# Sixteen-head landmark attention with a mixture of experts: the pseudo-inverse on a'a, the values carried through it

## The chip, the cores and the metric

One core of a Trainium2 chip runs the whole layer as one program. The metric is the device time of that core in microseconds. TensorE (PE) multiplies into PSUM, VectorE (DVE), ScalarE (ACT) and GpSimd (POOL) work beside it, and SyncE (SP) issues most transfers. The engines run their own instruction streams and meet only at semaphores.

## What is computed

The layer is an attention block and a mixture of eight experts, each with a norm ahead of it. The change lies in the attention, in the pseudo-inverse of a softmax matrix `attn2` of 64 x 64, one for each of 4 batches and 16 heads:

```python
def moore_penrose_inverse(a, iters=6):
    col = jnp.abs(a).sum(axis=-1); row = jnp.abs(a).sum(axis=-2)
    z = jnp.swapaxes(a, -1, -2) / (jnp.max(col) * jnp.max(row))
    for _ in range(iters):
        az = a @ z
        z = 0.25 * z @ (13 * I - az @ (15 * I - az @ (7 * I - az)))
    return z
...
attn2_inv = moore_penrose_inverse(attn2)
out = attn1 @ attn2_inv @ (attn3 @ v)
```

What is done with `attn1`, the convolution, the output product and the experts comes later in the program and isn't changed.

## The kernel before

The program has these stages: the norm of x and its transposes (to about 87 us of the profile); the landmarks and `c1`, 16 rounds of 4 heads in which sim3 is multiplied, its softmax taken and attn3 @ v built up (`c1_sim`, `c1_ut`, `c1_v3`, to 313 us); the pseudo-inverse (313 to 377 us); the landmark values and the products with w_fc and w_q (`landmark_values`, `g1_round`, 377 to 397.5 us); the token stage with softmax, convolution, output and routing (36 steps, from 397.5 us); the experts.

Two matrices of 64 x 64 lie over one another on the 128 partitions, so there are 32 pairs q, and a product of 64 x 64 uses one quarter of TensorE's array. The pairs are worked on in four groups of eight, and a turn of the iteration is four group steps, numbered n = 0 to 23. In the trace every product of fp32 operands has two records on PE and two on its weight load; counts of records are twice the counts of products.

The iteration of before keeps y = a z and w, the product of the factors, side by side in `yw`. For each n TensorE forms y y (`square`, 16 products of 64 columns), y (y y - 7 y + 15) (`cube`, the same) and factor times [y w] (`next_values`, 16 products of 128 columns), and `pair` interleaves the squares and cubes of two groups with the next values of the two groups before them. VectorE makes one pass over 512 elements per partition for each of `low_powers` (15 - 7 y, line 1054), `square` (line 1062) and `step_factor` (line 1068); ScalarE takes the next values out of PSUM in one instruction of 1024 elements (line 741). GpSimd does nothing in these turns. At the end `z_product` forms w zt, and `landmark_values` multiplies the values v3 with the inverse. The groups n and n + 1 use different banks of PSUM, and the order of every engine is written out by hand. GpSimd's stream is the all-reduce of the two maxima (line 553), the first w (line 556, waits for the first squares), four iotas (line 562), and the sum of `band` and `shift` (line 564) that the convolution of the token stage needs. `xd`, `band` and `shift` have nothing to do with the pseudo-inverse. `att`, the transposed `attn2`, is made in c1 at m = 4 and 5 by `a_transposed` (line 1512) and read by the squares of line 1563, ahead of `c1_ut(15, 0)`.

## Time and profile before

| | us |
|---|---|
| median of 3 runs | 1106.95 |
| range of the runs | 1105.58 to 1109.3 |
| span of the profiled execution | 1103.7 |
| median less span | 3.25 |
| PE busy in the span | 1063.5 |
| DVE, ACT, POOL busy | 644.0, 318.9, 300.6 |
| pseudo-inverse and landmark values, 313.4 to 397.5 | 84.1 |

The profile is one execution, with the time of every instruction. Busy times are shares of the span and an average over stages, so the stage that is changed is read by itself: its timeline by engine, and the view of busy time by stretch.

### The profile page before, as it was taken

Reading aid. Unit: us, or ns where it says so; the run is one execution under the profiler, and the core shown is the slowest. Engines: PE = TensorE matmul, PEld = TensorE weight load, DVE = VectorE, ACT = ScalarE, POOL = GpSimd, SP = SyncE. Lnnn points to the kernel's source line nnn. Section 1 sums busy time; section 2 is a strip of 40 time slices with the busy share of each in tenths; the row PEclk is TensorE's granted clock in tenths of the full one; section 3 lists DMA queues with packets and bytes.
Section 4 is the critical chain, followed back from the end, with each engine's and each line's share of the span. In section 5 each row is a group of like instructions: output and inputs, shape, how many; then the busy total and the mean of one; then the engine's idle time right before and its main releaser. Section 6 shows DMA issues by size and latency. Waiting matters only on the chain.

```text
span 1103.7 us, 22943 instructions
## 1 busy us (share of the span) xinstructions
PE 1063.5 (96%) x9126; PEld 854.5 (77%) x9126; DVE 644.0 (58%) x1376; ACT 318.9 (29%) x471; POOL 300.6 (27%) x303
## 2 busy tenths in 40 slices
PE   4999999999999999999999999999999999999996
PEld 4888888888888756666766766788887877878895
DVE  7457756565558576677677777875434334343332
ACT  4433233223324423322332332331222122121210
POOL 6000000000020013225525526563242333333333
PEclk9999999999999999999999999999999999999998
DMA  9300000000300050221422314335423233333122
GB/s 337 130 1 1 1 1 1 1 1 1 98 3 0 2 192 20 106 67 59 146 67 68 106 58 130 97 126 107 92 43 54 41 45 53 45 51 46 20 30 24
DMA packets 48252, 68.27 MB, mean 62 GB/s; under 512 B 8224, under 2 KB 41504, under 8 KB 47136
## 3 DMA queue, kind: packets, MB, share of 16 engines
q1 hardware_dynamic: 34288, 46.83, 13.7%
q0 software_dynamic: 13440, 16.93, 9.2%
q10 hardware_dynamic: 432, 3.24, 0.7%
q8 instruction: 62, 1.02, 0.4%
q14 instruction: 30, 0.25, 0.1%
HBM read 41.43 MB, written 26.59 MB: 62 GB/s over the span
## 4 chain that ended last, share of the span: by engine, by line
PE 84%; DVE 6%; issue 3%; POOL 3%; DMA 2%; ACT 1%; POOLq 0%; DVEq 0%; ACTq 0%
PE ps L1886 17%; PE ps L1482 10%; PE ps L1441 10%; PE ps L1785 9%; PE ps L1929 9%; PE ps L1732 8%; PE ps L1777 5%; PE ps L1870 2%; DMA out<-mem 2%; PE ps L1599 1%; PE ps L1849 1%; PE ps L1415 1%; PE ps L1618 1%; PE ps L1923 1%; PE ps L1497 1%
## 5 line engine op out<-in xcount | busy, mean ns | idle before, releaser
L1886 PE MATMUL ps<-mem 128*128 128x256 f32 (+1 forms) x1152 | 221.9, 345 | 0.0
L1886 PEld LDWEIGHTS ps<-mem 128*128 128x128 f32 x1152 | 190.1, 191 | 27.2 <-issue 7.5
L608 POOL DMA_INDIRECT out<-mem x60 | 101.8, 1697 | 187.9 <-DVE mem L1301 139.0
L1289 DVE TENSOR_TENSOR mem<-mem,ps 128x512 f32<-128x512 f32 x66 | 45.3, 687 | 147.3 <-PE ps L1886 129.6
L573 POOL TENSOR_TENSOR mem<-mem,small 128x1024 f32<-128x1024 f32 x36 | 68.7, 1907 | 223.9 <-DVE small L1223 119.4
L1732 PE MATMUL ps<-mem 128*128 128x512 f32 x288 | 129.4, 593 | 0.0
L821 ACT ACTIVATE mem<-ps 128x512 f32<-128x512 f32 x66 | 39.4, 597 | 275.5 <-PE ps L1886 247.4
L1785 PE MATMUL ps<-mem 128*128 128x256 f32 x512 | 118.4, 384 | 0.0
L1482 PE MATMUL ps<-mem 128*128 128x256 f32 x512 | 117.3, 382 | 0.6 <-ACT mem L695 0.6
L1441 PE MATMUL ps<-mem 128*128 128x256 f32 x512 | 114.7, 380 | 0.0
L1929 PE MATMUL ps<-mem 128*128 x480 | 113.7, 380 | 0.9 <-DVE mem L1289 0.9
L1785 PEld LDWEIGHTS ps<-mem 128*128 128x128 f32 x512 | 94.7, 190 | 14.7 <-issue 3.2
L1441 PEld LDWEIGHTS ps<-mem 128*128 128x128 f32 x512 | 95.5, 190 | 12.7 <-issue 0.3
L1482 PEld LDWEIGHTS ps<-mem 128*128 128x128 f32 x512 | 94.8, 190 | 13.5 <-issue 0.8
L1929 PEld LDWEIGHTS ps<-mem 128*128 128x128 f32 x480 | 88.3, 190 | 11.6 <-issue 1.1
L1732 PEld LDWEIGHTS ps<-mem 128*128 128x128 f32 x288 | 54.2, 190 | 54.8 <-issue 52.7
L587 POOL DMA_INDIRECT xs_d<-mem,idx x64 | 62.5, 977 | 54.3 <-DVE idx L1203 34.1
L1777 PEld LDWEIGHTS ps<-mem 128*64 128x64 f32 x1152 | 57.1, 137 | 20.7 <-issue 20.3
L1777 PE MATMUL ps<-mem 128*64 128x116 f32 x1152 | 65.1, 266 | 0.8 <-POOL mem L573 0.8
L1318 DVE COPY mem<-mem 128x2048 f32 x51 | 62.1, 1236 | 5.6 <-issue 3.2
L796 ACT ACTIVATE mem<-ps 128x928 f32<-128x928 f32 (+2 forms) x36 | 31.5, 875 | 111.5 <-PE ps L1777 111.5
L1301 DVE TENSOR_SCALAR mem<-ps,mem 128x256 f32<-128x256 f32 x66 | 29.7, 479 | 48.4 <-PE ps L1929 48.2
(239 smaller groups left out, 1382.1 us busy)
## 6 DMA issues: line engine op xcount, KB each, us to landing
mem<-w_gu SPq DMA_DIRECT2D x9, 1024.0 KB, 5.6
mem<-xs_d SPq DMA_DIRECT2D x22, 260.0 KB, 2.8
mem<-x SPq DMA_DIRECT2D x8, 512.0 KB, 8.2
mem<-x SPq DMA_DIRECT2D x32, 128.0 KB, 2.2
out<-mem SPq DMA_DIRECT2D x32, 128.0 KB, 1.7
mem<-w_down SPq DMA_DIRECT2D x8, 512.0 KB, 5.8
xnt_d<-mem ACTq DMA_DIRECT2D x3, 1056.0 KB, 5.2
mem<-xnt_d SPq DMA_DIRECT2D x3, 1056.0 KB, 6.2
```

Source lines behind the costliest of these rows:

```text
L573: pool.tensor_tensor(a1[:, u], ex[:, u].rearrange("p (h c) -> p h c", h=H), ri[:, 16 * u:16 * u + 16].unsqueeze(2).to_broadcast([P, H, M]) ...
L587: pool.indirect_dma_start(out=xs_d, out_offset=bass.IndirectOffsetOnAxis(ap=idx[:, u, v, c:c + 1].bitcast(U32), axis=0), in_=xd[:, u, v, c ...
L608: pool.indirect_dma_start(out=out_rows, out_offset=bass.IndirectOffsetOnAxis(ap=rows_to.bitcast(U32), axis=0), in_=ys[:, r % YRING], in_of ...
L1289: dve.tensor_tensor(hid[:, n % 2], sil[:, n % 2], bank(2 + n % 2), ALU.mult).then_inc(s("m_hid"), 1)
L1318: dve.tensor_copy(v, w_gu_s[:, e]).then_inc(s("m_w"), 1)
L1441: mm = pe.matmul(bank(t // 2)[:, t % 2 * 2 * P:(t % 2 + 1) * 2 * P], xnts[b][:, k, HALO + P * t:HALO + P * t + P], g3c[:, b, k, j * P:(j + ...
L1482: mm = pe.matmul(bank(6)[:, k * 2 * P:(k + 1) * 2 * P], xna[:, b, t, k * P:(k + 1) * P], e3s[m % 4][:, t], start=(t == 0), stop=(t == RT - 1))
L1732: mm = pe.matmul(bank(2 * u + half), xnt2[b % 2][:, k, TO * t:TO * t + P], g1c[:, b, k, 512 * half:512 * half + 512], start=(k == 0), stop ...
L1777: mm = pe.matmul(bank(4, 2)[c:c + 64, (h // 2) * P:(h // 2) * P + TO], a1[:, q % 2, h], band[:, h], start=True, stop=True)
L1785: mm = pe.matmul(bank(6)[:, 0:D], cvt[:, j, at_:at_ + P], pm[:, b, j], start=(j == 0), stop=(j == J - 1))
L1886: mm = pe.matmul(bank(2 * c + n % 2)[:, i * size:(i + 1) * size], w[:, k, c, f * P:(f + 1) * P], xst[:, a % 2, k, 0:size], start=(k == 0), ...
L1929: mm = pe.matmul(bank(down_bank(a, b))[:, 0:D], hid[:, u, i * size + b * P:i * size + (b + 1) * P], w_d_s[:, e, f], start=(f == 0), stop=( ...
```

## The change

The iteration now works on y = a'a (scaled), which needs no transpose, and on u = a' v3, the values, instead of w. With c = y - 3.5 (kept as `less`) a group step is two rounds of 16 products of 128 columns:

- `first(n)`: less times [y u], which gives y y - 3.5 y and the same for u. ScalarE takes it out in two instructions of 512, times 1/4, into `mw`, the y half first.
- `quadratic(n)`: VectorE makes `quad` = 4 times the y half of mw, plus 2.75, from SBUF to SBUF.
- `second(n)`: quad times mw.
- `next_values(n)`: VectorE sets yu = 27/32 yu - second in two passes of 512, the y half first, each with its own count in `i_yu`.
- GpSimd makes less for n + 4 from the y half, in one pass of 512, as soon as that half is counted.

It is the same polynomial: the quarter of (y y - 3.5 y + 2.75)(y y - 3.5 y) taken from 27/32 y is the quarter of y (13 - 15 y + 7 y y - y y y). In the last turn only the u half is formed, in products of 64 columns (`last_second`). Neither `z_product` nor the product with v3 is left; `landmark_values` transposes u.

In c1, `a_transposed` and its copies are gone; `column_sums` multiplies each a with one column of ones (64 products of 1 column) and VectorE takes the maximum from PSUM. The first squares move from m = 15 to m = 14. At m = 15 come `first_rows` (a' v3, 16 products of 64 columns for each of four groups, three of them here) and `first(0)` and `first(1)`.

The diff, cut:

```diff
+def last_bank(n):
+    return 2 if n == 4 * ITERS - 1 else 4 + 2 * (n % 2)
+
+
+def yu_count(n):
+    return 2 * min(n, 4 * (ITERS - 1)) + max(0, n - 4 * (ITERS - 1))
...
+        yu = at(SQ, 2 * HQ).rearrange("p (q c) -> p q c", q=NQ)
+        y_of, u_of = yu[:, :, 0:M], yu[:, :, M:2 * M]
+        mw = at(2 * SQ, 2 * 16 * M).rearrange("p (u q c) -> p u q c", u=2, q=8)
+        quad = at(2 * SQ + HQ, 2 * 8 * M).rearrange("p (u q c) -> p u q c", u=2, q=8)
+        less = at(3 * SQ, HQ).rearrange("p (q c) -> p q c", q=NQ)
...
-            pool.wait_ge(s("i_y0mm"), 4)
-            pool.tensor_scalar(w_of, eye1.unsqueeze(1).to_broadcast([P, NQ, M]), 1.0, 0.0, ALU.mult, ALU.add)\
-                .then_inc(s("i_w0"), 1)
+            for n in range(4 * ITERS):
+                gs = slice(8 * (n % 4), 8 * (n % 4) + 8)
+                if n < 4:
+                    pool.wait_ge(s("i_y0"), n + 1)
+                else:
+                    pool.wait_ge(s("i_yu"), 2 * (n - 4) + 1)
+                pool.tensor_tensor(less[:, gs], y_of[:, gs], eye_shift.unsqueeze(1).to_broadcast([P, 8, M]), ALU.subtract)\
+                    .then_inc(s("i_less"), 1)
 
...
+            def products_out(n):
+                act.wait_ge(s("i_first"), n + 1)
+                if n >= 2:
+                    act.wait_ge(s("i_second"), n - 1)
+                product = bank(2 * (n % 2), 2).rearrange("p (q c) -> p q c", q=8)
+                for c in (0, M):
+                    act.activation(mw[:, n % 2, :, c:c + M], product[:, :, c:c + M], ACT.Copy, scale=0.25).then_inc(s("i_mw"), 1)
...
+                if m == NP2 - 2:
+                    for g in range(4):
+                        first_values(g)
+            for g in range(3):
+                first_rows(g)
+            products_out(0)
+            products_out(1)
             c1_tokens_out(NP2 - 1)
-
-            for n in range(4 * ITERS):
...
-                act.wait_ge(s("i_zmm"), g + 1)
-                act.activation(zf[:, 8 * g:8 * g + 8], bank(g).rearrange("p (q c) -> p q c", q=8), ACT.Identity,
-                               scale=zz[:, 1:2]).then_inc(s("i_z"), 1)
+            products_out(2)
...
-                if m in (4, 5):
-                    b = 2 * (m - 4) + 1
-                    dve.wait_ge(s("b_at_tp"), b + 1)
-                    dve.tensor_copy(att[:, J * b:J * b + J], bank(7).rearrange("p (q c) -> p q c", q=J)).then_inc(s("b_at_dve"), 1)
+                if m == 4:
+                    dve.wait_ge(s("b_cols"), 1)
...
+            def quadratic(n):
+                dve.wait_ge(s("i_mw"), 2 * n + 1)
+                if n >= 2:
+                    dve.wait_ge(s("i_second"), n - 1)
+                dve.scalar_tensor_tensor(out=quad[:, n % 2], in0=mw[:, n % 2, :, 0:M], scalar=4.0,
+                                         in1=eye_quad.unsqueeze(1).to_broadcast([P, 8, M]),
+                                         op0=ALU.mult, op1=ALU.add).then_inc(s("i_quad"), 1)
+
+            def next_values(n):
                 gs = slice(8 * (n % 4), 8 * (n % 4) + 8)
...
+                dve.wait_ge(s("i_second"), n + 1)
+                product = bank(last_bank(n), 2).rearrange("p (q c) -> p q c", q=8)
+                for c in (0, M) if n < 4 * (ITERS - 1) else (M,):
+                    to = yu[:, gs, c:c + M]
+                    dve.scalar_tensor_tensor(out=to, in0=to, scalar=27.0 / 32, in1=product[:, :, c:c + M],
+                                             op0=ALU.mult, op1=ALU.subtract).then_inc(s("i_yu"), 1)
+
+            quadratic(0)
+            quadratic(1)
+            c1_values(NP2 - 1)
+            next_values(0)
+            for n in range(2, 4 * ITERS):
+                quadratic(n)
+                next_values(n - 1)
...
 
             dve.wait_ge(s("a_xnt_out"), 16 * (B - 1))
...
+            def column_sums():
+                pe.wait_ge(s("b_a"), B)
+                for q in range(NQ):
                     for r in halves:
-                        mm = pe.matmul(bank(6 + b % 2)[r, j * M:(j + 1) * M], zt[r, J * b + j], eye1[r], start=True, stop=True)
-                mm.then_inc(s("b_at_tp"), 1)
...
+            def first_rows(g):
+                pe.wait_ge(s("c1_v3"), 8 * g + 8)
+                for i in range(8):
+                    for r in halves:
+                        mm = pe.matmul(bank(g)[r, i * M:(i + 1) * M], zt[r, 8 * g + i], v3[r, 8 * g + i], start=True, stop=True)
+                mm.then_inc(s("i_u0mm"), 1)
...
+            spread = [i // 2 + 4 * (i % 2) for i in range(8)]
+
+            def crossed(h, i):
+                return halves[(h + i // 4) % 2]
+
+            def first(n):
+                for i in spread:
+                    q = 8 * (n % 4) + i
+                    for h in range(2):
+                        mm = pe.matmul(bank(2 * (n % 2), 2)[crossed(h, i), i * 2 * M:(i + 1) * 2 * M], less[halves[h], q],
+                                       yu[halves[h], q], start=True, stop=True)
+                mm.then_inc(s("i_first"), 1)
+
+            def second(n):
+                for i in spread:
+                    for h in range(2):
+                        mm = pe.matmul(bank(4 + 2 * (n % 2), 2)[crossed(h, i), i * 2 * M:(i + 1) * 2 * M], quad[halves[h], n % 2, i],
+                                       mw[halves[h], n % 2, i], start=True, stop=True)
+                mm.then_inc(s("i_second"), 1)
...
+            def last_second(n):
+                pe.wait_ge(s("i_mw"), 2 * n + 2)
+                pe.wait_ge(s("i_quad"), n + 1)
+                pe.wait_ge(s("i_yu"), yu_count(n - 1))
+                for i in spread:
+                    for h in range(2):
+                        mm = pe.matmul(bank(last_bank(n), 2)[crossed(h, i), (2 * i + 1) * M:(2 * i + 2) * M], quad[halves[h], n % 2, i],
+                                       mw[halves[h], n % 2, i, M:2 * M], start=True, stop=True)
+                mm.then_inc(s("i_second"), 1)
...
+            def turn(n, done):
+
+                wait_alone(pe, "i_less", done + n + 2)
+                first(n + 1)
+                wait_alone(pe, "i_mw", 2 * done + 2 * n + 2)
+                wait_alone(pe, "i_quad", done + n + 1)
+                wait_alone(pe, "i_yu", 2 * done + 2 * n - 2)
+                second(n)
...
-                    a_transposed(2 * m - 8)
-                    a_transposed(2 * m - 7)
+                if m == 4:
+                    column_sums()
                 if more:
                     c1_sim(2 * m + 5)
                 if m == 2:
                     pe.wait_ge(s("b_sub"), B)
...
+                if m == 4:
+                    pe.wait_ge(s("b_sums"), 1)
+                if m == NP2 - 2:
                     pe.wait_ge(s("c1_raw"), 2 * NP2)
                     for g in range(4):
-                        for i in range(8):
-                            for r in halves:
-                                mm = pe.matmul(bank(g)[r, i * M:(i + 1) * M], att[r, 8 * g + i], att[r, 8 * g + i], start=True, stop=True)
-                        mm.then_inc(s("i_y0mm"), 1)
-                if not last:
+                        first_square(g)
+                if m == NP2 - 1:
+                    pe.wait_ge(s("i_y0"), 4)
+                    for g in range(3):
+                        first_rows(g)
+                if m != NP2 - 2:
                     c1_sum_columns(m - 1)
                     c1_v3(m - 1)
                 c1_ut(m, 0)
                 if more and m > 1:
                     c1_max_columns(m + 2)
...
+                if m == NP2 - 1:
+                    c1_sum_columns(m)
+                    for n in range(2):
+                        pe.wait_ge(s("i_u0"), n + 2)
+                        first_ready(n)
...
+            second(0)
+            c1_v3(NP2 - 1)
+            first_ready(2)
+            first(2)
+            pe.wait_ge(s("i_mw"), 4)
+            first_rows(3)
+            pe.wait_ge(s("i_quad"), 2)
+            second(1)
+            pe.wait_ge(s("i_u0"), 4)
+            turn(2, 0)
+            turn(3, 0)
+            with pe.Fori(0, ITERS - 2) as it:
+                for n in range(4, 8):
+                    turn(n, 4 * it)
+            for n in range(4 * (ITERS - 1), 4 * ITERS - 1):
+                first_ready(n + 1)
+                first(n + 1)
+                last_second(n)
...
+            for n in range(4 * (ITERS - 1), 4 * ITERS - 1):
+                first_ready(n + 1)
+                first(n + 1)
+                last_second(n)
+            pe.wait_ge(s("w_in"), 16 * 3)
...
-            pe.wait_ge(s("w_in"), 16 * 3)
+            pe.wait_ge(s("i_yu"), yu_count(4 * ITERS - 2))
+            g1_round(0)
             landmark_values(0)
+            last_second(4 * ITERS - 1)
```

The order on the engines. VectorE in the steady part, before: three kinds of passes, of two groups at a time (1062 reads PSUM and SBUF, 1068 PSUM and the constants `eyes`, 1054 SBUF and `eyes`).

```order
L1062 TENSOR_TENSOR mem<-ps,mem 128x512 [waits i_squaremm,i_low] x2
L1068 SCALAR_TENSOR_TENSOR mem<-ps,eyes 128x512 [waits i_cubemm]
L1054 SCALAR_TENSOR_TENSOR mem<-mem,eyes 128x512 [waits i_yw]
L1068 SCALAR_TENSOR_TENSOR mem<-ps,eyes 128x512 [waits i_cubemm]
L1054 SCALAR_TENSOR_TENSOR mem<-mem,eyes 128x512 [waits i_yw]
```

VectorE in the same part, now: `quadratic` is line 1065 (SBUF and `eyes`, both in SBUF), `next_values` line 1075 (SBUF and PSUM).

```order
L1065 SCALAR_TENSOR_TENSOR mem<-mem,eyes 128x512 [waits i_second,i_mw]
L1075 SCALAR_TENSOR_TENSOR mem<-mem,ps 128x8x64 [waits i_second]
L1075 SCALAR_TENSOR_TENSOR mem<-mem,ps 128x8x64
L1065 SCALAR_TENSOR_TENSOR mem<-mem,eyes 128x512 [waits i_second,i_mw]
L1075 SCALAR_TENSOR_TENSOR mem<-mem,ps 128x8x64 [waits i_second]
L1075 SCALAR_TENSOR_TENSOR mem<-mem,ps 128x8x64
```

Three passes for a group step stand there as before; two of them are now the two halves of the last step.

GpSimd between the all-reduce and the token stage, before (`ISA` is no arithmetic):

```order
L556 TENSOR_SCALAR mem<-eyes 128x32x64 [waits i_y0mm]
L562 IOTA mem 128x8 [waits band_in]
L562 IOTA mem 128x8 [waits pool_chain] x3
L564 TENSOR_TENSOR mem<-mem,shift 128x1856 [waits pool_chain]
L573 TENSOR_TENSOR mem<-mem,small 128x1024 [waits c2_rinv,bfc_in]
```

GpSimd now; line 567 is `less`, 573 and 575 are the iotas and the sum of band and shift.

```order
L567 TENSOR_TENSOR mem<-mem,eyes 128x512 [waits i_y0] x4
L567 TENSOR_TENSOR mem<-mem,eyes 128x512 [waits i_yu] x20
L573 IOTA mem 128x8 [waits band_in]
L573 IOTA mem 128x8 [waits pool_chain] x3
L575 TENSOR_TENSOR mem<-mem,shift 128x1856 [waits pool_chain]
L584 TENSOR_TENSOR mem<-mem,small 128x1024 [waits c2_rinv,bfc_in]
```

The iotas and the sum of band and shift have moved from ahead of the iteration to behind the 24 passes of `less`.

## Rows read from the trace of the kernel before

**Rows 1.** The page, its first line and its chain that ended last.

```profile
span 1103.7 us, 22943 instructions
...
PE 84%; DVE 6%; issue 3%; POOL 3%; DMA 2%; ACT 1%; POOLq 0%; DVEq 0%; ACTq 0%
```

**Rows 2.** Busy time by stretch, one pair of group steps; columns in its first line.

```profile
core 0: us, PE busy (x) PEld busy (x) DVE busy (x) ACT busy (x) POOL busy (x), PEclk, DMA share, GB/s
340.24:344.90 4.66, 4.41 (x204) 4.06 (x198) 3.88 (x7) 2.05 (x2) 0.00 (x0) 1.00 0.00 0
```

**Rows 3.** Timeline of VectorE, the same pair; start, duration, engine, line.

```profile
340.24 1.45 DVE L1062 TENSOR_TENSOR mem<-ps,mem 128x512 f32<-128x512 f32 x2
342.26 0.69 DVE L1068 SCALAR_TENSOR_TENSOR mem<-ps,eyes 128x512 f32<-128x512 f32 x1 [0.57 <-PE ps L1599]
342.87 0.68 DVE L1054 SCALAR_TENSOR_TENSOR mem<-mem,eyes 128x512 f32<-128x512 f32 x1
```

**Rows 4.** Timeline of TensorE, the first cube behind it.

```profile
341.07 0.28 PE L1599 MATMUL ps<-mem 64*64 64x64 f32 x2
```

**Rows 5.** Timeline of TensorE, the last rounds of c1.

```profile
292.12 0.38 PE L1464 MATMUL ps<-ids,small 128*128 128x128 f32 x2
293.06 3.69 PE L1482 MATMUL ps<-mem 128*128 128x256 f32 x16 [0.56 <-ACT mem L695]
296.59 0.38 PE L1472 MATMUL ps<-ids,mem 128*128 128x128 f32 x2
...
301.17 3.95 PE L1563 MATMUL ps<-mem 64*64 64x64 f32 x128
```

**Rows 6.** Timeline of ScalarE, the last token copy of c1.

```profile
313.29 0.60 ACT L695 ACTIVATE mem<-ps 128x512 f32<-128x512 f32 x1 [7.38 <-PE ps L1482]
```

**Rows 7.** Timeline of TensorE, landmark values to the first token matmul.

```profile
379.10 1.09 PE L1719 MATMUL ps<-mem 64*64 64x256 f32 x16
380.02 0.63 PE L1689 MATMUL ps<-mem 64*64 64x64 f32 x16
380.58 1.14 PE L1700 MATMUL ps<-mem 64*128 64x256 f32 x8
...
397.53 2.81 PE L1732 MATMUL ps<-mem 128*128 128x512 f32 x6
```

**Rows 8.** Timeline of TensorE, transposes in c1 and products of 8 columns.

```profile
138.61 2.08 PE L1512 MATMUL ps<-eyes,mem 64*64 64x64 f32 x64
140.62 3.72 PE L1441 MATMUL ps<-mem 128*128 128x256 f32 x16
...
702.70 0.96 PE L1761 MATMUL ps<-rw,mem 128*128 128x8 f32 x8
```

**Rows 9.** GpSimd, timeline and one line by source (ns min/median/max).

```profile
307.11 0.78 POOL L562 IOTA mem<- 128x8 int32 x4
307.97 4.12 POOL L564 TENSOR_TENSOR mem<-mem,shift 128x1856 f32<-128x1856 f32 x1
...
L579 POOL TENSOR_TENSOR mem<-mem,bfc x32: 720/729/739, 423.6 to 709.7; 128x256 f32<-128x256 f32 x32
```

**Rows 10.** GpSimd and VectorE side by side, then three lines by source.

```profile
512.82 1.92 POOL L573 TENSOR_TENSOR mem<-mem,small 128x1024 f32<-128x1024 f32 x1
...
513.11 1.72 DVE L1165 SCALAR_TENSOR_TENSOR mem<-logits 128x32 f32<-128x32 f32 x1
...
L1165 DVE SCALAR_TENSOR_TENSOR mem<-logits x9: 175/193/1786, 476.7 to 732.0; 128x32 f32<-128x32 f32 x7, 128x16 f32<-128x16 f32 x2
...
L1213 DVE TENSOR_TENSOR mem<-ps,small x36: 1223/1224/1225, 402.6 to 699.2; 128x1024 f32<-128x1024 f32 x36
...
L1220 DVE TENSOR_REDUCE small<-mem x36: 1206/1220/1221, 404.9 to 703.6; 128x16 f32<-128x1024 f32 x36
```

**Rows 11.** Timeline of TensorE's weight loads that wait for no engine.

```profile
324.10 0.13 PEld L1618 LDWEIGHTS ps<-mem 64*64 64x64 f32 x1 [1.42 <-issue]
...
375.01 0.13 PEld L1620 LDWEIGHTS ps<-mem 64*64 64x64 f32 x2 [1.50 <-issue]
```

220 lines of the change are left out of this document (45 added, 175 removed).

## The prediction

> **What bounds the kernel now.** Read the page first: TensorE is busy 96% of the span and 84% of the chain that ended last is its own [rows 1]. The changed stage is two parts of that chain. In c1 TensorE has work without a gap but for 0.56 us at 292.5 [rows 5], so there only TensorE's own work counts. In the iteration the share is lower. The busy time by stretch shows for one pair of group steps 4.66 us, with PE 4.41 and DVE 3.88, at full clock [rows 2]. The timeline says who is late: VectorE starts line 1068 only after 0.57 us of waiting for the cubes, and TensorE starts the next cubes at 341.07, 0.14 after line 1062's first pass ends at 340.93 [rows 3, 4]. So the pair runs in a ring, PE to DVE to PE and over ACT, and each engine waits a little. One group step is 2.33 us. There are twelve such pairs, the first and the last with other work.
>
> **The change, part by part.** All times are on the clock of the profiled execution; the first token matmul starts at 397.53 there, and nothing behind it is changed.
>
> *c1, m = 4 and 5.* Four groups of transposes go, 2.01 us for each two of them (138.61 to 140.62), so 4.03 in all. The column sums are 64 products, 128 records, of one column. No row has that form. The records of 64 columns come every 29 ns (3.95 us less 0.22 for 128 records) [rows 5], so 3.7 us; from below, the pair's 204 records in 4.41 us (22 ns) [rows 2] give 2.8; from above, the products with 8 columns come every 100 ns (0.96 less 0.26, over 7) [rows 8] with twice the weight columns on the whole array, which for halves one after the other gives 6.4. I take 3.7, as its weights have the same form: a gain of 0.3, between a gain of 1.2 and a loss of 2.4. VectorE's maximum over 32 columns has the 3.5 us of the next `c1_sim` as cover. Its dropped copy and sum lay beside TensorE's work.
>
> *c1, m = 14 and 15.* On the clock: both versions finish `c1_max_rows(15)` at 292.43. Squares 4 x 0.93 = 3.73, to 296.16; they cover the 0.56 of waiting. Half of `c1_ut` takes 3.53 (293.06 to 296.59); sums, `c1_v3` and the other half 4.58 (296.59 to 301.17), of which 0.93 and about 0.1 of switching aren't the half: 304.2 [rows 5]. Three groups of a'v3, 2.80; sums and v3 0.93; half 3.55; sums 0.31 (292.12 to 292.43 for the same form): 311.8. `first(0)`, `first(1)`: 16 products of 128 columns over four quarters of the array are the same columns for a quarter as 16 of 64 over two, so 0.93 each: 313.6. Last half: 317.16. The last token copy starts 0.20 behind it and takes 0.60 [rows 6], `c1_v3` follows after 0.15 and takes 0.62, VectorE scales it (about 0.7 with the handover), and the first pass of `next_values(0)` starts at 319.4. The four early `less` passes and the copies lie under c1; the wait for them is met by some 9 us.
>
> *One group step.* TensorE: two times 0.93, 1.87. VectorE: three passes; such passes start 0.60 apart and take 0.69 (342.26 and 342.87) [rows 3], so 1.80. ScalarE: two of 512, 0.60 each [rows 6], 1.1. So by engine time a step would be 1.87 in place of 2.33. GpSimd decides otherwise. `less` reads two tensors of SBUF. The line 564 sum of the same form is 4.12 us for 1856 elements, line 579 0.73 for 256 [rows 9]; the straight line between them gives 2.12 ns an element and 1.27 us for 512. Its bounds: 1.13, from line 573 (1024 elements, 1.92, one input repeated over the inner dimension) [rows 10] and line 579, and 1.46, two times line 579. And it doesn't run beside VectorE's quadratic. Look at the token stage: GpSimd's line 573 runs from 512.82 to 514.74. VectorE issues line 1165, which reads two SBUF tensors of 32 elements, at 513.11, and it is done at 514.83, after 1.72 us; undisturbed it takes 0.19 [rows 10]. Four of its seven calls of this size fall into a GpSimd pass and all four end 0.07 to 0.09 behind it. Line 1213, with one input from PSUM and one from SBUF, takes 1.22 to 1.23 all 36 times, 16 of them inside a GpSimd pass [rows 10]. So a VectorE pass with both inputs in SBUF stands still until GpSimd's pass ends, and one with a PSUM input doesn't. `quadratic` has both in SBUF (mw and eyes); `next_values` has PSUM.
>
> The Trainium skill, "SBUF — State Buffer", section "SBUF: two separate sides", states this: the port pair of VectorE and GpSimd is a lock for a whole instruction, and it takes VectorE's two-input passes against a GpSimd pass that reads SBUF. By this rule the step is the 2.55 worked out next, without it the 1.87 above.
>
> The ring is then: the quadratic starts at 0, the y half of `next_values` at 0.60, ends at 1.29, GpSimd starts 0.08 later, runs 1.27 to 2.64, and the next quadratic, waiting since 1.80, starts in effect 0.10 before that end (it ends 0.09 behind with 0.19 of its own): **2.55 us** a step, where 2.33 stood. It holds every time, because `less` is always released by the y half. TensorE has 0.7 us to spare in it and so has ScalarE. The bounds of `less` make it 2.41 to 2.74.
>
> *To the end of the turns.* The y half of step 19 starts at 319.4 + 19 x 2.55 = 367.85. The last `less` starts 0.77 later and ends at 369.89. Now the moved work of GpSimd comes: four iotas, and after 0.83 us (307.11 to 307.97, as before) the sum of band and shift, from 370.72 to 374.84, 4.12 us [rows 9], again with two SBUF inputs. `quadratic(22)` is due at 369.79 + 1.20 = 370.99, 0.27 behind the start of that sum. It stands until 374.74. That costs 3.75 us on the path, since the u half of step 21 and TensorE's next product are queued behind it. Then: u half from 375.34 to 376.03, TensorE 0.14 later, `g1_round(0)` 1.06, `landmark_values` 0.56, the last second round of half width 0.47, `landmark_values` 0.56: the first product with w_fc at 378.82. In before it is at 379.10, the first token matmul 18.43 later at 397.53, eight rounds of 2.54 that don't change [rows 7]. So 397.25: **0.3 us earlier**.
>
> *Waits for code.* In before TensorE's loads stand in this stage without a releaser, longest for 1.42 us at 324.10 and 1.50 at 375.01 [rows 11]; with smaller ones that is 3 to 4 us of the 105.1 from 292.43. Here TensorE issues 128 records and loads in 2.55 us where it issued 384 in 4.66, and its 0.7 of spare time for a step covers most of such a wait. I take 0, with 0 to 2 as bounds.
>
> *Sum.* 0.3 and 0.3 of c1: 0.6 less than the span of 1103.7, 1103.1. The median of the runs is 3.25 above the span of its profile: **1106.4**. The unknown `less` moves it through 20 steps, by 2.8 down (1103.6) and 3.8 up (1110.2); the column sums by 0.9 down and 2.7 up; code by 2 up.
>
> **The rivals.**
>
> *The lock does not bite.* Then a step is 1.87 and the band sum costs nothing on the path: 19 x 0.68 + 3.75 = 16.7 less, of which waits for code, no longer covered, take back up to 4. I put it at 1092. For it speaks only that four calls of a tiny pass are not passes of 512; against it, all four.
>
> *The next values are stopped too* (the other side). Line 1213 has PSUM as its first input, `next_values` has SBUF first, and no row here shows that order beside GpSimd. If it stops, the u half waits for `less`: 0.69 + 0.08 + 1.27 - 0.10 + 0.60 + 0.60 = 3.14 a step, 19 x 0.59 = 11.2 more: 1117.6. It decides as soon as `less` outlasts a u half that has started behind it; against it, line 1220, whose only input lies in SBUF, is never stopped either (1.21 to 1.22 in 36 calls) [rows 10], and neither half reads two SBUF tensors.
>
> *GpSimd's pass is dearer,* from its eight rows of 64 with a stride of 128: at 1.6 us a step is 2.88, 20 x 0.33 = 6.6 more: 1113. Line 564 had 16 rows of 116 and lies on the line that I used, which speaks against it.
>
> *The order dodges part of it.* If quadratic(22) comes 0.3 us sooner, it starts ahead of the band sum, and only quadratic(23) stands, 2.8 us instead of 3.75, with the second rounds already issued ahead: about 1.5 less, and with the lower bound of `less` 1101.5.
>
> *The change doesn't do what it says:* it does remove the third round of products (96 products in a pair become 64), but not their columns, 4096 a group step before and now. If TensorE were paced by instructions and not by columns, this would pay; at 29 ns a record for two quarters it is paced by columns. That is in the 1.87 already.
>
> **How the numbers follow.** A measurement of this kernel can tell about 0.3%, 3.3 us. The forecast, with the lock and `less` within its bounds: 0.58, of it 0.12 below 1103.6, 0.34 within, 0.12 above 1110.3. No lock: 0.11. Next values stopped: 0.08. A dearer pass: 0.10. The dodge: 0.13, most of it (0.09) below 1103.6. Faster 0.32, same 0.38, slower 0.30. The range leaves out no lock and the stopped next values, 0.19 together, and reaches from 1099, the lower bounds of `less` and the column sums with the dodge, to 1114, the dearer pass with a little code.
>
> **What would show it.** In the profile after: `quadratic` lasts not 0.69 but about 1.4 in its records, and each ends 0.6 behind a `less`; the step is 2.55; ScalarE and TensorE wait each step; GpSimd's sum of band and shift starts near 370.7 and one quadratic beside it lasts over 4 us; the first token matmul is at 397.3. If quadratics last 0.69 beside `less`, the lock is wrong and the time is near 1092. If the u halves last over 1 us, it is near 1117. If `less` is not 1.27, the step moves by the same amount.

## The result: 0.23% slower, where a time 0.05% below before was forecast

| | before | after |
|---|---|---|
| median of 20 runs each, us | 1106.01 | 1108.84 |
| range of the runs | 1104.08 to 1109.3 | 1105.19 to 1112.28 |
| span of the profiled execution | 1103.7 | 1105.2 |
| TensorE busy in it | 1063.5 | 1060.1 |
| VectorE, ScalarE, GpSimd busy | 644.0, 318.9, 300.6 | 653.5, 321.1, 328.3 |
| first token matmul starts at | 397.53 | 399.09 |

The ratio of the times is 1.0023, with a 95% interval of 1.0016 to 1.0031: slower by 0.16 to 0.31%. The forecast was 1106.4 us, 0.05% below 1106.95, the median of before that was known then. The measured time lies 2.4 us above it and on the other side of before. After the first token matmul both profiles take 706.1 or 706.2 us, so the difference of the two profiled executions, 1.5 us, lies wholly ahead of it. The medians differ by 2.8; where the other 1.3 us come from is a question for the experiments.

The page after, its first line, TensorE's busy time and the chain that ended last. TensorE has lost 3.4 us of work and the chain has moved to VectorE, to 8% from 6% in [rows 1]:

```profile
span 1105.2 us, 21500 instructions
PE 1060.1 (96%) x8358; PEld 849.7 (77%) x8358; DVE 653.5 (59%) x1369; ACT 321.1 (29%) x493; POOL 328.3 (30%) x325
PE 82%; DVE 8%; issue 4%; POOL 3%; DMA 2%; ACT 1%; POOLq 0%; DVEq 0%; ACTq 0%
```

**The group step.** Timeline of VectorE in the stretch that answers to [rows 3] (start, duration, engine, line; 1065 is `quadratic`, 1075 `next_values`, 567 `less`):

```profile
340.93 1.27 DVE L1075 SCALAR_TENSOR_TENSOR mem<-mem,ps 128x512 f32<-128x512 f32 x2
342.12 1.38 DVE L1065 SCALAR_TENSOR_TENSOR mem<-mem,eyes 128x512 f32<-128x512 f32 x1
343.43 1.27 DVE L1075 SCALAR_TENSOR_TENSOR mem<-mem,ps 128x512 f32<-128x512 f32 x2
```

Timeline of GpSimd beside it:

```profile
341.68 1.27 POOL L567 TENSOR_TENSOR mem<-mem,eyes 128x512 f32<-128x512 f32 x1 [1.23 <-DVE mem L1075]
```

GpSimd's pass runs from 341.68 to 342.95. VectorE's quadratic is issued at 342.12 into it and ends at 343.50, 0.55 behind its end. The two halves of `next_values`, of which the second runs beside the same pass, keep their 0.68. A step is 2.50 us. By line over the whole stretch (ns, least, median and most), where [rows 3] had 0.68 and 0.69 for the passes of before:

```profile
L1065 DVE SCALAR_TENSOR_TENSOR mem<-mem,eyes x24: 677/1381/4405, 314.9 to 376.4; 128x512 f32<-128x512 f32 x24
L1075 DVE SCALAR_TENSOR_TENSOR mem<-mem,ps x44: 673/675/687, 320.9 to 380.0; 128x512 f32<-128x512 f32 x44
L567 POOL TENSOR_TENSOR mem<-mem,eyes x24: 1265/1276/1282, 298.3 to 369.2; 128x512 f32<-128x512 f32 x24
```

**The end of the turns.** The quadratic of 4.41 us on VectorE's timeline:

```profile
371.52 4.41 DVE L1065 SCALAR_TENSOR_TENSOR mem<-mem,eyes 128x512 f32<-128x512 f32 x1
```

The sum of band and shift on GpSimd's, which it outlasts by 0.55:

```profile
371.27 4.11 POOL L575 TENSOR_TENSOR mem<-mem,shift 128x1856 f32<-128x1856 f32 x1
```

And TensorE's, which waits for it (line 1560 is `last_second(22)`, 1683 `g1_round(0)`):

```profile
376.03 0.69 PE L1560 MATMUL ps<-mem 64*64 64x64 f32 x32 [3.35 <-issue]
376.67 1.35 PE L1683 MATMUL ps<-mem 64*128 64x256 f32 x8
```

**What nobody had in the sum: the clock.** The profile of before has TensorE's granted clock at 1.00 (2.4 GHz) up to the last few microseconds. The profile of after has two stretches at 0.50 (1.2 GHz). One lies right behind the column sums, one behind TensorE's 3.35 us without work. Busy time by stretch of after; the granted clock is the third number from the end:

```profile
core 0: us, PE busy (x) PEld busy (x) DVE busy (x) ACT busy (x) POOL busy (x), PEclk, DMA share, GB/s
142.10:145.40 3.30, 3.30 (x11) 2.66 (x11) 0.19 (x1) 0.00 (x0) 0.00 (x0) 0.51 0.00 0
145.40:147.30 1.90, 1.90 (x11) 1.62 (x10) 0.00 (x0) 0.00 (x0) 0.00 (x0) 1.00 0.00 0
377.20:380.90 3.70, 3.70 (x76) 3.10 (x76) 1.97 (x4) 1.12 (x4) 0.00 (x0) 0.54 0.02 4
```

The same places in before:

```profile
142.00:149.00 7.00, 7.00 (x48) 5.97 (x47) 2.78 (x7) 1.02 (x1) 0.00 (x0) 1.00 0.00 0
377.00:384.00 7.00, 7.00 (x126) 5.32 (x122) 3.93 (x6) 3.92 (x11) 0.00 (x0) 1.00 0.01 2
```

On the timeline, the 16 records of `c1_sim` behind the column sums take 5.29 us; in [rows 8] the same 16 take 3.72:

```profile
138.25 3.97 PE L1515 MATMUL ps<-ones,mem 64*64 64x1 f32 x128
142.15 5.29 PE L1444 MATMUL ps<-mem 128*128 128x256 f32 x16
```

TensorE is busy through the whole of the column sums, 3.90 of 3.90 us in the stretch from 138.20 to 142.10, and the clock falls all the same.

Laid beside the forecast, the profiled execution of after is 2.1 us longer than the span of 1103.1 that was worked out:

| piece | forecast | measured | later than forecast |
|---|---|---|---|
| `c1_max_rows(15)` against before's 292.12 | 0.30 earlier | 293.00, 0.88 later | +1.2 |
| from there to the y half of `next_values(0)` | 27.3 | 27.9 (to 320.92) | +0.6 |
| first to last `less` of the 20, 19 steps | 48.45 | 47.50 (321.68 to 369.18) | -0.95 |
| last `less` to the first w_fc product | 10.2 | 11.2 (to 380.37) | +1.0 |
| w_fc product to the first token matmul | 18.43 | 18.72 (to 399.09) | +0.3 |

### The profile page after: what moved, and what is told of

It reads as the page before. It is cut to its first block, busy times and chain, and to the rows that moved or that the text cites. A ratio compares the mean times of both kernels' runs of the same rounds, so it can differ in the third digit from the quotient of the medians.

```text
span 1105.2 us, 21500 instructions
## 1 busy us (share of the span) xinstructions
PE 1060.1 (96%) x8358; PEld 849.7 (77%) x8358; DVE 653.5 (59%) x1369; ACT 321.1 (29%) x493; POOL 328.3 (30%) x325
## 3 DMA queue, kind: packets, MB, share of 16 engines
q8 instruction: 62, 1.02, 0.4%
## 4 chain that ended last, share of the span: by engine, by line
PE 82%; DVE 8%; issue 4%; POOL 3%; DMA 2%; ACT 1%; POOLq 0%; DVEq 0%; ACTq 0%
PE ps L1872 17%; PE ps L1485 10%; PE ps L1444 10%; PE ps L1771 9%; PE ps L1915 9%; PE ps L1718 8%; PE ps L1763 5%; PE ps L1856 2%; DMA out<-mem 2%; DVE mem L1075 2%; PE ps L1835 1%; PE ps L1418 1%; PE ps L1909 1%; PE ps L1500 1%; PE ps L1683 1%
## 5 line engine op out<-in xcount | busy, mean ns | idle before, releaser
L567 POOL TENSOR_TENSOR mem<-mem,eyes 128x512 f32<-128x512 f32 x24 | 30.5, 1275 | 181.9 <-ACT mem L715 140.3
```

## The experiments

Theory: (1) VectorE's quadratic stands still while GpSimd's pass runs, because both read two SBUF tensors, and this sets the step and the stall at the end; (2) the surplus over the forecast is TensorE's clock, which falls behind the one-column products and behind the stall. Rivals: the 1.38 us belong to the quadratic itself; the slow products are waits or switches of tile shape. Every kernel was timed beside the kernel of before on the same chip. Single executions differ by some microseconds, so where the question is a piece of the timeline, the traces are compared.

**Does the clock fall because of the one-column products?** The same products with 64 columns of ones, each overwriting 63 columns of the one ahead.

```diff
-mm = pe.matmul(bank(7)[r, q:q + 1], zt[r, q], ones[r, 0:1], start=True, stop=True)
+mm = pe.matmul(bank(7)[r, q:q + M], zt[r, q], ones[r, 0:M], start=True, stop=True)
```

> The changed kernel with one difference: each of the 64 column-sum products multiplies with 64 columns of ones in place of 1 and writes 64 columns, of which the next product overwrites 63. The sums are the same numbers. In the changed kernel these 128 records take 3.97 us at 1 column and the 16 records of the sim3 products right behind them take 5.29 us where 3.72 is usual, with a granted clock of 0.50 for about 3 us. Theory (the clock falls because the 1-column products leave TensorE's array nearly empty): the 128 records still take about 4.0 us, the sim3 round behind them goes back to 3.7, the granted clock stays at 1.00, and c1_max_rows(15) starts near 291.4 instead of 293.0; the time is about 1.5 us less than the changed kernel's. Rival (the round behind is slow for another reason, such as the wait for VectorE's maximum or the switch of tile shape): 5.3 us stays and the time does not change.

Measured: 1106.84 us, ratio to before 0.9999 (0.9990 to 1.0008), where the changed kernel has 1.0023. The column sums by source, with 64 columns:

```profile
L1515 PE MATMUL ps<-ones,mem x128: 218/218/267, 138.3 to 142.0; 64*64 64x64 f32 x128
```

The same line of the changed kernel, with 1 column:

```profile
L1515 PE MATMUL ps<-ones,mem x128: 193/193/243, 138.2 to 142.0; 64*64 64x1 f32 x128
```

With 64 columns again, busy time in the stretch of these products and in the one behind it:

```profile
138.20:142.10 3.90, 3.90 (x129) 3.81 (x128) 0.69 (x1) 1.85 (x2) 0.00 (x0) 1.00 0.02 4
142.10:145.70 3.60, 3.60 (x21) 3.11 (x18) 0.19 (x1) 0.00 (x0) 0.00 (x0) 1.00 0.00 0
```

And `c1_sim` behind them on its timeline:

```profile
142.13 3.72 PE L1444 MATMUL ps<-mem 128*128 128x256 f32 x16
```

128 records take the same time with 64 columns as with one: they are paced at 30 ns each by something that both share, not by their columns. But with 64 columns the clock stays at 1.00, the 16 records of `c1_sim` take 3.72 us, and the first token matmul comes at 397.52 instead of 399.09: 1.57 us from the clock, as expected. `c1_max_rows(15)` is at 291.43 (expected 291.4). The rival falls. The other traces bear it out: the clock falls behind the column sums in all eight executions with products of one column, and in none of the nine without them. The Trainium skill ("TensorE: Matmul & The Clock Gate", "What's actually happening") says that the chip sets this clock by how busy the engine has been; here the engine's busy share was full in both kernels, and the clock falls only in the one whose products have one column. A busy time without a gap in the profile is thus no sign that the clock stays.

**Does the stall make the clock fall at the end?** TensorE gets 26 products to do in it, whose result nobody reads.

```diff
                 first(n + 1)
+                if n == 4 * ITERS - 2:
+                    pe.wait_ge(s("i_mw"), 2 * n + 2)
+                    for i in range(13):
+                        for h in range(2):
+                            pe.matmul(bank(h)[halves[h], 0:2 * M], v3[halves[h], 0],
+                                      v3[halves[h], 0:2], start=True, stop=True)
                 last_second(n)
```

> The changed kernel with 26 added products of 128 columns whose result nobody reads (v3 times v3 into banks 0 and 1, two quarters of the array), placed between first(23) and last_second(22), where TensorE has nothing to do for 3.35 us because quadratic(22) stands still beside GpSimd's sum of band and shift. They should end just before quadratic(22) does, at about 375.7. Theory (the idle stretch makes the clock fall, which is then at 0.50 from about 377.7 to 380.7): with the stretch filled the clock stays at 1.00, and from the end of quadratic(22) to the first w_fc product it takes about 3.2 us instead of 4.4; about 1.1 us less in all. Rival (the end is slow through waits or switches of tile shape): nothing gained, or a loss if the added products outlast the stall.

Measured: 1108.54 us, ratio 1.0014 (1.0005 to 1.0023). The trace says more, since the low stretch behind the column sums was longer in this execution than in the first (the sims took 6.59 us) and moved all that follows by 1.7 us. The added products and the next real one on the timeline:

```profile
374.13 3.03 PE L1666 MATMUL ps<-mem 64*64 64x128 f32 x52
377.72 0.69 PE L1560 MATMUL ps<-mem 64*64 64x64 f32 x32 [0.55 <-issue]
```

Busy time in the stall and behind it:

```profile
373.30:378.00 4.70, 4.15 (x112) 3.94 (x108) 4.70 (x2) 1.09 (x2) 3.77 (x1) 1.00 0.01 3
378.00:382.00 4.00, 4.00 (x127) 3.40 (x119) 2.87 (x7) 1.33 (x4) 0.00 (x0) 1.00 0.02 4
```

From `last_second(22)` to the first token matmul it takes 21.53 us (377.72 to 399.25) instead of 23.06 (376.03 to 399.09), 1.5 less, where 1.1 was expected. So 1.5 us is what the low clock costs there. That the added products are what kept the clock up isn't shown by this one execution, since the unfilled stall doesn't always bring it down. Six traces have the 3.35 us without work: in four the clock falls, in the kernel of the next experiment and in one further execution of the changed kernel it doesn't, and both of these take 21.54 us as well. Nor do the times settle it, since the intervals of the two ratios overlap. That the stall is the cause of the fall is shown better from the other side: five kernels below have no such stall, and in none of their traces is the clock low there.

**Column sums the other way round.** The ones are stationary and a moves, 512 columns at a time.

```diff
+            def column_sums(k):
+                for g in range(2):
+                    for h in range(2):
+                        mm = pe.matmul(bank(6 + g)[halves[(h + g) % 2]], ones[halves[h], 0:M],
+                                       zt[halves[h], 8 * (2 * k + g):8 * (2 * k + g) + 8], start=True, stop=True)
...
+                if m in (4, 5):
+                    dve.wait_ge(s("b_cols"), m - 3)
+                    dve.tensor_reduce(zz[:, m:m + 1], bank(6, 2), AX, ALU.max).then_inc(s("b_max"), 1)
```

> The changed kernel with the column sums made the other way round: the ones are the stationary matrix and a moves, 8 products of 512 columns, four at m = 4 and four at m = 5, over all four quarters of the array, into banks 6 and 7; VectorE takes a maximum over 1024 columns twice. By columns each four cost 0.93 us, 1.9 in all in place of 3.97, and with no stretch of one-column products the clock stays at 1.00, so that c1_max_rows(15) starts 3.6 us earlier than the changed kernel's 293.0, at 289.4. Rival: two of the quarters wait for the other two and each four cost 1.9 us: 1.8 us earlier from the clock and little more. A second rival: VectorE's maximum of 1.2 us is late for c1_ut and gives some of it back.

Measured: 1106.17 us, ratio 0.9994 (0.9985 to 1.0003). Both lots on TensorE, and the wait behind the second:

```profile
138.21 1.09 PE L1518 MATMUL ps<-mem,ones 64*64 64x512 f32 x8
...
154.71 1.09 PE L1518 MATMUL ps<-mem,ones 64*64 64x512 f32 x8
155.73 3.72 PE L1447 MATMUL ps<-mem 128*128 128x256 f32 x16
160.13 0.44 PE L1478 MATMUL ps<-ids,mem 128*128 128x128 f32 x2 [0.67 <-DVE small L1040]
```

Each lot takes 1.02 us to the next line, 2.04 in place of 3.90, and the clock stays up. `c1_max_rows(15)` is at 290.63, 2.4 us earlier than in the changed kernel, not the 3.6 expected; 0.67 of the difference is the second rival (TensorE waits for VectorE's maximum at m = 5), the rest isn't attributed. The first token matmul is at 395.18, 3.9 us earlier: besides the 2.4 it has 1.5 from the clock, which didn't fall behind the stall in this execution.

**The sum of band and shift at another place.** It moves from behind the last `less` to between `less(3)` and `less(4)`.

```diff
             for n in range(4 * ITERS):
+                if n == 4:
+                    pool.wait_ge(s("c1_sum"), NP2)
+                    pool.wait_ge(s("band_in"), 16)
...
+                    pool.tensor_tensor(band, band, shift[:, :].unsqueeze(1).to_broadcast([P, H, TO]), ALU.add)\
+                        .then_inc(s("band_ok"), 1)
```

> The changed kernel with GpSimd's four iotas and the sum of band and shift placed between less(3) and less(4), behind VectorE's last sums of c1, so at about 305.8 to 310.8, where VectorE has only passes with an input from PSUM and small ones. Lock theory: quadratic(22) takes 1.38 us like the others instead of 4.41, 3.0 us less; TensorE's idle stretch of 3.35 us goes and with it the low clock behind it, 1.1 us more: about 4.1 us less than the changed kernel, near 1104.7. If the 4.41 us of quadratic(22) had another cause it stays and nothing is gained.

Measured: 1104.05 us, ratio 0.9977 (0.9966 to 0.9988), faster than both. All quadratics by source:

```profile
L1067 DVE SCALAR_TENSOR_TENSOR mem<-mem,eyes x24: 677/1379/1386, 314.9 to 373.3; 128x512 f32<-128x512 f32 x24
```

Busy time in the stretch where the clock had been low:

```profile
376.00:381.00 5.00, 5.00 (x84) 3.71 (x82) 3.52 (x6) 1.88 (x7) 0.00 (x0) 1.00 0.01 3
```

The longest quadratic is 1.39 us, and the first token matmul is at 393.94, 5.15 us earlier: 3.6 from the stall and 1.5 from the clock behind it.

**Is it a lock, and is it the quadratic's two SBUF inputs?** The quadratic takes its input from PSUM. ScalarE takes the same banks out behind VectorE.

```diff
-                dve.wait_ge(s("i_mw"), 2 * n + 1)
+                dve.wait_ge(s("i_first"), n + 1)
-                dve.scalar_tensor_tensor(out=quad[:, n % 2], in0=mw[:, n % 2, :, 0:M], scalar=4.0,
+                product = bank(2 * (n % 2), 2).rearrange("p (q c) -> p q c", q=8)
+                dve.scalar_tensor_tensor(out=quad[:, n % 2], in0=product[:, :, 0:M], scalar=1.0,
...
             def products_out(n):
-                act.wait_ge(s("i_first"), n + 1)
+                act.wait_ge(s("i_quad"), n + 1)
```

> The changed kernel with quadratic(n) reading the y half of the product from PSUM (times 1, plus 2.75) instead of 4 times mw from SBUF, the same numbers; ScalarE takes the product out behind it, since both may not read one bank at once. No VectorE pass of the iteration then has two inputs in SBUF. Lock theory: the pass takes about 0.68 us each time although GpSimd's less runs beside it, the group step falls from 2.50 to about 1.87 to 1.95 us (TensorE's two rounds of 0.93 or VectorE's three passes of 0.6), the sum of band and shift stops nobody, and the first token matmul comes 14 to 17 us earlier than 399.09; near 1093. Rival (the 1.38 us of quadratic are its own, from the constant or the strides, or port traffic and not a lock): the step stays at 2.5 and the added wait of ScalarE makes it slower.

> The kernel above with GpSimd's sum of band and shift placed between less(3) and less(4) as well. Lock theory: once no VectorE pass has two SBUF inputs, that sum costs nothing at either place, so the time is within 0.5 us of the kernel above. If the sum also delays passes that read PSUM, this kernel is 1 to 3 us faster.

Measured: 1101.77 us, ratio 0.9953 (0.9941 to 0.9966), and with the band sum early too 1103.22, ratio 0.9964 (0.9951 to 0.9977). The quadratic by source (the first kernel):

```profile
L1066 DVE SCALAR_TENSOR_TENSOR mem<-ps,eyes x24: 681/683/691, 314.3 to 371.2; 128x512 f32<-128x512 f32 x24
```

One step of it on VectorE's timeline:

```profile
343.29 1.29 DVE L1076 SCALAR_TENSOR_TENSOR mem<-mem,ps 128x512 f32<-128x512 f32 x2 [0.28 <-PE ps L1551]
344.49 0.68 DVE L1066 SCALAR_TENSOR_TENSOR mem<-ps,eyes 128x512 f32<-128x512 f32 x1
```

On ScalarE's:

```profile
345.21 1.08 ACT L729 ACTIVATE mem<-ps 128x512 f32<-128x512 f32 x2 [1.08 <-DVE mem L1066]
```

On TensorE's:

```profile
346.74 1.10 PE L1551 MATMUL ps<-mem 64*64 64x128 f32 x32 [0.19 <-issue]
```

The lock theory holds: all 24 quadratics last 0.68 to 0.69, those beside `less` and the one beside the 4.14 us of the band sum too. The forecast of the gain doesn't: the first token matmul is at 392.64, 6.4 us earlier and not 14 to 17, and the step is 2.40 us (321.67 to 367.30 in 19 steps), not 1.9. One of these steps takes 3.36, the last 16 take 2.33 each. By the order of the engines a new ring has taken the place of the lock: `next_values` is done at 344.58, the quadratic issued behind it at 344.49 is done at 345.17, ScalarE's two passes at 346.29, and the second round starts at 346.74, two steps after the one that fed those halves. With ScalarE behind VectorE and the quadratic behind both halves, two steps thus cost 4.7 us. The rows alone don't prove this ring, since TensorE's own first round also ends only 0.19 before 346.74. The last experiment tests it. The earlier band sum changes nothing in the trace once no quadratic can be stopped: the low stretch behind the column sums was longer in that execution (the last rounds of c1 start 1.69 later), and with that taken off its first token matmul is at 392.42 beside 392.64. The two medians differ by 1.4 us, more than the expected 0.5; their intervals overlap, and the low stretches of single executions differ by as much.

**Is it GpSimd's reading?** Three further kernels: the kernel of before with a GpSimd pass of 512 added for each factor, which reads two SBUF tensors, one, or none, and writes to unused memory. `low_powers` (two SBUF inputs) is line 1060 here.

```diff
+            for n in range(4 * ITERS - 2):
+                pool.wait_ge(s("i_factor"), n + 1)
+                pool.tensor_tensor(scratch[:, n % 4], v3[:, 0], eye13.unsqueeze(1).to_broadcast([P, 8, M]), ALU.subtract)
```

In the other two the last line is

```diff
+                pool.tensor_scalar(scratch[:, n % 4], v3[:, 0], 2.0, 0.0, ALU.mult, ALU.add)
```

or

```diff
+                pool.memset(scratch[:, n % 4], 1.0)
```

> The kernel before with one added GpSimd pass of 128 x 512 for each factor, released by the factor pass (line 1068), just as VectorE starts low_powers (line 1054, one input in SBUF, the constant eyes in SBUF too). The added pass reads two SBUF tensors. It writes to unused memory, and nobody reads it. Lock theory: low_powers ends about 0.1 us behind the GpSimd pass and takes 1.3 to 1.4 us instead of 0.69, lines 1062 and 1068 (PSUM input) keep 0.69, and GpSimd's pass takes 1.27. No lock: 0.69 throughout.

> The same with an added GpSimd pass that reads one SBUF tensor (times 2). If any GpSimd pass that reads SBUF stops VectorE's pass with two SBUF inputs, low_powers lasts as long as the GpSimd pass, by about 0.1 us more; if only a pass with two inputs does, it keeps 0.69.

> The same with an added GpSimd memset of 128 x 512, which reads nothing. If the lock needs a GpSimd pass that reads SBUF, low_powers keeps 0.69 us; if every GpSimd pass that touches SBUF takes the port, it lasts as long as the memset.

By source, `low_powers` and GpSimd's pass, with two inputs:

```profile
L1060 DVE SCALAR_TENSOR_TENSOR mem<-mem,eyes x24: 671/684/1161, 314.0 to 368.5; 128x512 f32<-128x512 f32 x24
L571 POOL TENSOR_TENSOR mem<-mem,eyes x22: 1648/1690/1723, 317.9 to 368.8; 128x512 f32<-128x512 f32 x22
```

With one:

```profile
L1060 DVE SCALAR_TENSOR_TENSOR mem<-mem,eyes x24: 671/683/1100, 314.0 to 370.5; 128x512 f32<-128x512 f32 x24
L571 POOL TENSOR_SCALAR mem<-mem x22: 620/990/1002, 318.0 to 370.5; 128x512 f32<-128x512 f32 x22
```

With none:

```profile
L1060 DVE SCALAR_TENSOR_TENSOR mem<-mem,eyes x24: 672/682/693, 314.4 to 367.4; 128x512 f32<-128x512 f32 x24
L571 POOL MEMSET mem<- x22: 525/526/526, 318.4 to 367.3; 128x512 f32 x22
```

With a GpSimd pass that reads, one or two tensors alike, a `low_powers` that starts into it is stretched (to 1.10 and 1.16 at most), and a GpSimd pass that starts into `low_powers` is stretched too: 0.62 becomes 1.00, and with two inputs it is 1.69 where the same form took 1.27 in the changed kernel. So either engine can be the one that stands. With the memset neither is. The expected 1.3 to 1.4 us for `low_powers` didn't come, because it was often first and GpSimd stood instead. The times of single executions were 1108.52, 1110.95 and 1106.52 us, with 1105.02 for the kernel of before beside them. The engines thus don't meet only at semaphores, as was said at the start: here one stands for the other and no semaphore shows it. The Trainium skill, "SBUF — State Buffer", section "SBUF: two separate sides", which the prediction named, says that the one that starts first has the port pair for its whole instruction; these runs and the trace of after agree with it.

**All three, and one step more.** The last kernel also puts `quadratic(n + 2)` between the y half and the u half of `next_values(n)`.

```diff
                 for c in (0, M) if n < 4 * (ITERS - 1) else (M,):
+                    if c == M and n < 4 * ITERS - 2:
+                        quadratic(n + 2)
                     to = yu[:, gs, c:c + M]
```

> The changed kernel with all three: quadratic from PSUM, the sum of band and shift early, and the column sums with the ones stationary. If the savings lie one behind the other they add: 14 to 17 us for the iteration and its end and 3.6 us for the column sums, near 1089 to 1091.

> The kernel with all three (quadratic from PSUM, band sum early, ones stationary) and one more difference: on VectorE, quadratic(n + 2) stands between the y half and the u half of next_values(n) instead of behind both. With all three the group step was still 2.3 us: the quadratic of PSUM waits for both halves, ScalarE for the quadratic, and second(n + 2) for ScalarE: 0.93 + 0.25 + 1.21 + 0.68 + 0.05 + 1.08 + 0.45 = 4.65 for two steps. With the quadratic 0.6 earlier the ring is 4.05, so a step of 2.0 us instead of 2.3, about 6 us less than the kernel with all three, near 1093.5. Rival (TensorE's waits for code or ScalarE set the step now): the step stays at 2.3 and the time near 1099.5.

Measured: 1099.48 us, ratio 0.9935 (0.9921 to 0.9948), where 1089 to 1091 was expected, and 1097.14 us, ratio 0.9908 (0.9891 to 0.9924), where 1093.5 was. The last is 0.9% faster than the kernel of before and 1.1% faster than the changed one. The savings do add: with all three the first token matmul is at 390.19, 8.9 us earlier, of which 2.4 come from the column sums and 6.4 from the quadratic, the stall at the end among them. It was the size of the parts that the expectation had too large. Timeline of a step, all engines:

```profile
342.19 0.69 DVE L1071 SCALAR_TENSOR_TENSOR mem<-ps,eyes 128x512 f32<-128x512 f32 x1
342.79 0.68 DVE L1083 SCALAR_TENSOR_TENSOR mem<-mem,ps 128x512 f32<-128x512 f32 x1
...
342.91 1.08 ACT L731 ACTIVATE mem<-ps 128x512 f32<-128x512 f32 x2 [0.89 <-DVE mem L1071]
...
343.36 1.10 PE L1551 MATMUL ps<-mem 64*64 64x128 f32 x32
344.63 1.10 PE L1558 MATMUL ps<-mem 64*64 64x128 f32 x32 [0.17 <-issue]
```

The quadratic stands ahead of the u half and ScalarE starts behind it. The step is 2.23 us (319.32 to 361.76 in 19), beside 2.40 for the kernel with the three. Of the 0.3 a step by which the ring was shortened, 0.17 came, where 2.0 us a step was expected. What is late now is TensorE itself: ScalarE is done at 343.99, but the first round that TensorE started at 343.36 (line 1551) lasts to 344.46, and the second round follows it after 0.17. From the second round before it, at 342.46, that makes 2.17 us. So the quadratic's place in VectorE's order did cost time, as the ring says, and the next limit is TensorE's own two rounds with such pauses. No run shows what the pauses are, and none reached the 1.87 of the prediction.

**The same two kernels again.** Four further executions, unchanged, for their clock.

> The changed kernel itself, once more, for the places where TensorE's clock is low in another execution. The first trace had it at 0.50 from 142 to 145.3 (behind the one-column products) and from 377.3 to 380.8 (behind the stall of quadratic(22)) and nowhere else before the end, with a span of 1105.2; the median of its runs is 1.9 longer. If the clock explains that, a longer execution shows a longer low stretch behind the column sums (some 6.6 us instead of 3.3) or one near 720, and the rest of the timeline is the same to 0.3 us.

> The changed kernel itself, a further execution: a low clock behind the column sums in every execution, with a length that varies; behind the stall of quadratic(22) and near 720 in some. Span = 1097 plus half the length of the low stretches ahead of the end, to within 1 us.

> The changed kernel itself, the third further execution: again a low clock behind the column sums, 3.3 or 6.6 us long, with or without a stretch near 377 and near 720.

> The kernel of before, a further execution: no low clock ahead of 700; near 720 perhaps, since that stage is the same in both kernels, and then a span about 1.6 us longer than 1103.7.

The spans are 1109.5, 1107.1 and 1110.1 for the changed kernel and 1104.8 for before. Busy time by stretch in the first of them:

```profile
142.00:145.50 3.50, 3.50 (x31) 3.12 (x31) 0.19 (x1) 0.00 (x0) 0.00 (x0) 0.50 0.00 0
145.50:149.00 3.50, 3.50 (x11) 2.79 (x11) 0.00 (x0) 0.00 (x0) 0.00 (x0) 0.58 0.00 0
377.00:384.00 7.00, 5.92 (x110) 5.00 (x113) 4.31 (x7) 1.04 (x3) 0.43 (x1) 0.51 0.01 2
```

In the second, where the clock doesn't fall behind the stall:

```profile
377.00:384.00 7.00, 6.36 (x159) 5.16 (x162) 5.60 (x10) 2.31 (x7) 0.00 (x0) 1.00 0.02 5
```

In before again:

```profile
377.00:384.00 7.00, 7.00 (x134) 5.47 (x132) 3.64 (x6) 4.21 (x11) 0.00 (x0) 1.00 0.01 2
```

Read in stretches of 1 us up to 1090, TensorE's clock is at half speed for 6.8 us in the first execution of the changed kernel, and for 13.7, 10.2 and 17.0 in these; in before and before again for none. Behind the column sums it is low in all four, for 3.4 us in the first and 6.8 in the others; behind the stall in three of four, for 3.4 us once and 6.8 twice; near 722 in two. From `last_second(22)` to the first token matmul the four take 23.06, 24.15, 21.54 and 24.02 us: the one without a low clock there is the short one, by the same program. With half of these lengths taken off, the four spans are 1101.8, 1102.7, 1102.0 and 1101.6: the same kernel, but for the clock. The expectation named 1097 as that base, which was wrong: it had counted the low stretch at the very end, which both kernels have. The low stretch near 722 didn't show in the two traces of before, but it does in the one with two inputs added and in the one with one input; it belongs to both kernels' common part. Over all timed runs of the changed kernel the mean granted clock has a median of 0.992, over those of before 0.997. And among the 20 timed runs the span goes with that clock: 1103.6 and 1104.3 us at 0.996, 1110.5 at 0.989.

## Why the prediction was wrong

**What held.** That VectorE's quadratic is stopped by `less`: 1.38 us and 0.55 behind its end, forecast about 1.4 and 0.6. That `less` takes 1.27: it does (1.265 to 1.282). That the next values aren't stopped: 0.673 to 0.687 in all 44. That the step goes from 2.33 to 2.55: to 2.50. That the band sum stops `quadratic(22)`: it lasts 4.41 us, forecast about 4.4 with its own 0.69. So both large terms, about 4 us each against what is saved elsewhere, came out within 1 us. The rivals "no lock", "next values stopped too" and "dearer `less`" fell, and so did the dodge, by little: the quadratic was issued 0.25 us behind the start of the band sum, forecast 0.27.

**What failed.** The sum had a place for everything except TensorE's clock. It is a sum of small differences, -0.6 us in all, and the clock alone costs 3.1 us in the profiled execution: 1.57 behind the column sums (the kernel with 64 columns) and 1.5 behind the stall (the executions in which it didn't fall there). Without it the span would be 1102.1, 1.0 below the forecast of 1103.1 and on the forecast side of before's 1103.7. The step that failed in c1 is the term for the column sums, "a gain of 0.3, between a gain of 1.2 and a loss of 2.4". The products themselves took 3.90 us against 3.7 forecast; what the term left out is what such products do to the products behind them: `c1_max_rows(15)` starts at 293.00, and with the clock up at 291.43, where 291.82 was forecast. The step that failed at the end is "`g1_round(0)` 1.06, `landmark_values` 0.56, the last second round of half width 0.47": the first took 1.28 and the last 1.0, as the clock fell during the first (it is low from about 377.4), behind the very wait that the prediction had worked out to be 3.75 us. The prediction priced the wait and didn't ask what TensorE does when it comes back from it.

**Why the median is worse than the profile.** "The median of the runs is 3.25 above the span of its profile" was carried over from before. Each timed run lists its span, and time less span is 1.69 to 1.78 in all 20 runs of the changed kernel; the rest of the 3.25 was the difference of two executions, from the median of only three runs. Over the 20 runs it is 2.3 for before and 3.6 for the changed kernel, so of the 2.4 us by which the forecast was low, 2.1 lie in the profiled execution and the rest in this term. In the changed kernel the difference isn't constant: its low stretches are longer or more in most executions than in the profiled one. That is the other 1.3 us between the medians, as far as four traces and the mean clock of the timed runs can say.

**Smaller terms.** From `c1_max_rows(15)` to the first `next_values` it took 0.6 more than forecast; it grows in pieces of 0.03 to 0.15 in the part of c1 where small and full tile shapes alternate, for which the prediction had 0.1 once. The steps gave 0.95 back, since 2.50 isn't 2.55. The 0 for waits for code held, in that all 19 steps take 2.49 to 2.51. One sentence of the prediction isn't borne out, though no term hung on it: "at 29 ns a record for two quarters it is paced by columns". A record takes 30 ns with 64 columns and with one, and in a round of 128 columns over four quarters 28 (32 records from 341.39 to 342.29), so at this size the number of records counts at least as much.

## What to carry to other kernels

A term of a sum has to say what TensorE's clock is behind it: a stretch of products of one column, or a wait of some microseconds that an edit creates, costs once in itself and can cost again in the work that follows at half speed. Here the first did so in every execution, the second in four of six. Whether unused products put into the wait gain time is open. A VectorE pass with both inputs in SBUF shouldn't run beside a GpSimd pass that reads SBUF; taking one input from PSUM is enough, but look for the next ring before counting the whole gain, since here a quadratic shorter by 0.7 us in each step gave only 0.1, and moving one pass within VectorE's order another 0.17. Where a median and a profile differ, compare executions before the difference is carried into a forecast.

## What the runs showed that was not expected

- 128 records of one column take 3.90 us and of 64 columns 3.90 us (30 ns each), and only the former bring the clock to half, although TensorE is busy without a gap in both.
- The length of such a low stretch differs between executions of the same program: 3.4 us in one and 6.8 in three, with the same work behind the column sums.
- The same wait of 3.35 us brought the clock down in four executions and not in two, one of these of the same program.
- A GpSimd pass is stretched by VectorE's two-input pass as well: 0.62 to 1.00 us and 1.27 to 1.69 us.
- Half of the column sums takes 1.02 us as eight records of 512 columns over four quarters of the array, and 1.95 as 64 records of one column.
